# Turning attention outputs and expert products with transposing DMAs instead of TensorE

## What is computed

```python
x = x + 0.5 * ffn(layernorm(x))      # ternary weights, 128 -> 512 -> 128, relu
x = x + attn0(layernorm(x))          # rmsnorm, 16 heads of 64, causal, sigmoid gate per head
x = x + 0.5 * ffn(layernorm(x))
x = x + 0.5 * moe(layernorm(x))      # 8 experts, each token to its top 2
x = x + attn1(layernorm(x))          # layernorm, 16 heads of 64, causal
x = x + 0.5 * moe(layernorm(x))
```

## Time and profile before

| | us |
|---|---|
| median of three executions | 967.55 (967.09 to 970.55) |
| the profiled execution, its span from first to last instruction | 1000.9 |

### The profile page before, as it was taken

How to read it: one execution, slowest core, us unless ns; L and a number is a source line. 1 busy time by engine, 2 the same in 40 slices (tenths; PEclk the granted TensorE clock), 3 DMA queues, 4 the chain that set the end, 5 groups by cost and what they waited for, 6 DMA issues and landing times.

```text
span 1000.9 us, 33897 instructions
## 1 busy us (share of the span) xinstructions
PE 897.1 (90%) x13160; PEld 640.5 (64%) x13160; DVE 792.1 (79%) x2394; ACT 673.5 (67%) x1183; POOL 734.7 (73%) x685
## 2 busy tenths in 40 slices
PE   5789999999999879899987899999999985998884
PEld 3467676776777656566654676777677764666663
DVE  6889898888889877777656889888888887866563
ACT  6688888878877626556555787767767762545552
POOL 6789989889887745666545999878888883666662
PEclk9999999999999979999999999999999997999997
DMA  5201011010030001122111000000000001121222
GB/s 153 78 10 45 3 45 45 3 45 2 3 107 3 2 20 39 52 43 85 38 30 51 3 3 3 12 3 2 13 3 3 13 2 30 41 43 44 86 62 82
DMA packets 21118, 33.79 MB, mean 34 GB/s; under 512 B 4578, under 2 KB 10466, under 8 KB 20964
## 3 DMA queue, kind: packets, MB, share of 16 engines
q1 hardware_dynamic: 13728, 18.50, 5.9%
q0 software_dynamic: 5888, 12.07, 4.8%
q10 hardware_dynamic: 1348, 1.05, 0.3%
HBM read 22.44 MB, written 9.18 MB: 32 GB/s over the span
## 4 chain that ended last, share of the span: by engine, by line
PE 63%; DVE 18%; ACT 6%; issue 6%; POOL 3%; another core or an unknown queue 2%; DMA 1%; SPq 0%; POOLq 0%; DVEq 0%; ACTq 0%
PE ps L1698 8%; PE ps L1889 8%; PE ps L1700 8%; PE ps L1699 7%; DVE arena L1308 4%; PE ps L1919 3%; PE ps L2128 3%; PE ps L1853 3%; PE ps L1920 3%; PE ps L1921 3%; PE ps L2140 2%; PE ps L2141 2%; PE ps L2142 2%; PE ps L1864 2%
## 5 line engine op out<-in xcount | busy, mean ns | idle before, releaser
L784 POOL TENSOR_TENSOR arena<-arena 128x1024 f16<-128x1024 f32 x190 | 344.9, 1816 | 86.2 <-ACT arena L980 75.9
L1308 DVE CUSTOM_DVE_ANT_0 arena<-ps,mask_qk 128x512 bf16<-128x512 f32 (+3 forms) x512 | 224.4, 485 | 25.0 <-PE ps L1853 23.8
L972 ACT ACTIVATE arena<-ps,lift 128x1024 f32<-128x1024 f32 (+1 forms) x192 | 186.7, 972 | 85.0 <-PE ps L1899 82.2
L1889 PE MATMUL ps<-arena 64*128 64x512 f16 (+3 forms) x1536 | 148.5, 299 | 10.2 <-ACT arena L972 6.8
L835 POOL DMA_INDIRECT arena<-x_rows,arena x92 | 92.6, 1006 | 88.5 <-PE ps L2103 43.7
L1919 PE MATMUL ps<-arena 128*128 128x65 f16 x1280 | 130.9, 195 | 0.2 <-DVE arena L1332 0.2
L1920 PE MATMUL ps<-arena 128*128 128x64 f16 x1280 | 130.4, 193 | 0.0
L1921 PE MATMUL ps<-arena 128*128 128x65 f16 x1280 | 130.0, 194 | 0.0
L843 POOL DMA_INDIRECT y_rows<-arena x92 | 90.8, 987 | 49.0 <-ACT arena L1138 26.1
L1919 PEld LDWEIGHTS ps<-arena 128*128 128x128 f16 x1280 | 117.4, 98 | 8.4 <-issue 0.5
L1920 PEld LDWEIGHTS ps<-arena 128*128 128x128 f16 x1280 | 117.9, 99 | 0.2 <-issue 0.2
(11 more groups left out here) (288 smaller groups left out, 2695.9 us busy)
## 6 DMA issues: line engine op xcount, KB each, us to landing
stage<-in_L_ffn_W SPq DMA_DIRECT2D x4, 1024.0 KB, 5.3
arena<-y_rows SPq DMA_DIRECT2D x14, 256.0 KB, 3.6
x_rows<-XN SPq DMA_DIRECT2D x8, 256.0 KB, 2.1
arena<-x_rows,arena POOLq DMA_INDIRECT x92
y_rows<-arena POOLq DMA_INDIRECT x92
stage<-in_L_attn_Wkv SPq DMA_DIRECT2D x2, 512.0 KB, 8.3
X<-in_L_attn_tokens SPq DMA_DIRECT2D x3, 256.0 KB, 5.1
out_x<-X SPq DMA_DIRECT2D x3, 256.0 KB
```

The lines of the kernel that those rows point to most:

```text
L784: g.tensor_tensor(PL[:, b, :, cols], P32[:, :, cols], PH[:, b, :, cols], ALU.subtract).then_inc(s_pl, 1)
L972: a_.activation(P32[:, :, UNIT_AT[u]:UNIT_AT[u] + UNIT_W[u]], ps[:, 4:6, 0:UNIT_W[u]], ACT.Exp, bias=lift[:]).then_inc(s_ex_p, 1)
L1308: v_.tensor_tensor_reduce(masked[:, x, 0:w], ps[:, 2 + x, at:at + w], mask_qk[:, CH - w:CH], 1.0, NEG, ALU.add, ALU.max, accum_out=MX[:, i ...
L1889: mm(ps[:, 4 + x, at:at + w], keys, queries, start=(n_ == 0 and part == 0), stop=False)
```

## The change

1. Attention: `turn_outputs` goes. ACT `output_high` writes the high part of O32 into OS right at the turn's start, ahead of `exps(0)`; DVE `output_low` writes the rest, ahead of `maxima(0)`. SP issues one transposing DMA of 128x1024 float16 (both parts) into OT, which lies in T32; `project_out` waits for it.
2. Experts: `turned_product` goes. ACT and DVE split G32 itself into GS (three buffers), in step t-2; SP turns both parts with one transposing DMA into GT (four buffers, a semaphore each); the down product moves from lag 3 to lag 4. ACT takes `product_high` ahead of `gate`, DVE `product_low` ahead of `product`. The freed PSUM banks 3 and 4 double the banks of the up products.
3. The YS ring has eight buffers in place of four, in another place of the arena, and POOL waits for the last scatters before it writes there in the second attention.
4. SP's other DMAs are spread over the turns and steps, between the transposing ones.

```diff
-        GRING = 3
+        GRING = 4
+        SRING = 3
         XRING = 4
-        YRING = 4
+        YRING = 8
...
-        OTh = carve([CH], F16)
-        OTl = carve([CH], F16)
+        OS = carve([2, CH], F16)
+        OT = T32[:].bitcast(F16).rearrange("p (k i d) -> p k i d", k=2, i=TPB)
...
-        TLAGS = (0, 1, 2, 3)
+        DOWN_LAG = 4
...
+        def up_banks(t):
+
+            return 1 + 2 * (t % 2), 2 + 2 * (t % 2)
...  (SP)
+            def attention(a):
...
+                def body(t):
+                    o = items(t)[4]
+                    if o is not None:
+                        j = base + o
+                        sp.wait_ge(s_o_lo, j + 1)
+                        if j >= 1:
+                            sp.wait_ge(s_op_ps, j)
+                        sp.dma_start_transpose(OT.rearrange("p k i d -> p (k i) d"), OS.rearrange("p k c -> p (k c)")
+                                               ).then_inc(s_o_turned, 16)
+                    if a == 0 and t == 0:
+                        expert_block(0)
...
+            def moe(m):
+
+                for t in range(ETILES):
+                    w = ETILES * m + t
+                    sp.wait_ge(s_g_lo, w + 1)
+                    if t >= GRING:
+                        sp.wait_ge(s_y_ps, w - GRING + 1)
+                    sp.dma_start_transpose(GT[:, t % GRING].rearrange("p k f d -> p (k f) d"),
+                                           GS[:, t % SRING].rearrange("p k h -> p (k h)")
+                                           ).then_inc(s_g_turned[t % GRING], 16)
+                    if m == 0 and t == 4:
+                        rows_out(3, 2)
...
+                    if t == 31:
+                        results_in(m, 0)
...  (ACT)
+                    def output_high():
                         j = base + o
-                        act.wait_ge(s_ot_ps, j + 1)
-                        if o >= 1:
-                            act.wait_ge(s_op_ps, j)
-                        a_.activation(OTh, ps[:, 7, :], ACT.Copy).then_inc(s_oth_sb, 1)
+                        act.wait_ge(s_o_ev, j + 1)
+                        if j >= 1:
+                            act.wait_ge(s_o_turned, 16 * j)
+                        a_.activation(OS[:, 0], O32.rearrange("p a x d -> p (a x d)"), ACT.Copy).then_inc(s_o_hi, 1)
...
+                    if o is not None:
+                        output_high()
                     if s is not None:
                         exps(0)
...
                 def product_high(t, w):
-                    act.wait_ge(s_gt_ps, w + 1)
-                    if t >= GRING:
-                        act.wait_ge(s_y_ps, w - GRING + 1)
-                    a_.activation(GH[:, t % GRING].rearrange("p a b -> p (a b)"), ps[:, 3 + t % 2, :], ACT.Copy
-                                  ).then_inc(s_g_hi, 1)
+                    act.wait_ge(s_g32_rdy, w + 1)
+                    if t >= SRING:
+                        act.wait_ge(s_g_turned[(t - SRING) % GRING], moved(m, (t - SRING) % GRING, t - SRING + 1))
+                    a_.activation(GS[:, t % SRING, 0], G32[:, t % 2, :], ACT.Copy).then_inc(s_g_hi, 1)
...
-                run_tiles(m, (token_high, gate, product_high, result), carried)
+                run_tiles(m, ((token_high, 0), (product_high, 2), (gate, 1), (result, DOWN_LAG)), carried)
...  (DVE)
+                    if o is not None:
+                        output_low()
                     if m is not None:
                         maxima(0)
...
-                run_tiles(m, (token_low, product, product_low, None), carried)
+                run_tiles(m, ((token_low, 0), (product_low, 2), (product, 1)), carried)
...  (PE)
-                    def turn_outputs():
...
                     def project_out():
-                        pe.wait_ge(s_otl_sb, base + o + 1)
+                        pe.wait_ge(s_o_turned, 16 * (base + o + 1))
...
-                def turned_product(t, w):
...
                 def down(t, w):
                     g, e = t % GRING, offsets[t]
-                    pe.wait_ge(s_g_lo, w + 1)
+                    pe.wait_ge(s_g_turned[g], moved(m, g, t + 1))
...
-                run_tiles(m, (turned_token, up, turned_product, down), carried)
+                run_tiles(m, ((turned_token, 0), (up, 1), (down, DOWN_LAG)), carried)
```

More of the change, by code:

```diff
@@ L530, in macaron_block @@
         KEY_AT = {k: UNIT_AT[u] + at for u, unit in enumerate(EXP_UNITS) for k, at in unit}
-        TLAGS = (0, 1, 2, 3)
+        DOWN_LAG = 4
         OUT_LAG = 8
         def run_tiles(m, stages, carried):
-            for t in range(ETILES + TLAGS[-1]):
-                for f, lag in zip(stages, TLAGS):
-                    if f is not None and 0 <= t - lag < ETILES:
+            for t in range(ETILES + DOWN_LAG):
+                for f, lag in stages:
+                    if 0 <= t - lag < ETILES:
                         f(t - lag, ETILES * m + t - lag)
                 carried(m, t)
+        def up_banks(t):
+            return 1 + 2 * (t % 2), 2 + 2 * (t % 2)
         def second_weights(i):
@@ new lines, in rows_out, with results_in @@
+            def rows_out(n, c):
+                sp.wait_ge(s_ln_xn, NORM_NO[n, c])
+                at = c % HCH * CH
+                sp.dma_start(x_rows[c // HCH][at:at + CH].rearrange("(p t) d -> p t d", t=TPC),
+                             XN[:, TPC * c:TPC * (c + 1), :]).then_inc(s_x_rows[c // HCH], 16)
+            def results_in(m, h):
+                for k in range(YRING):
+                    sp.wait_ge(s_y_out[k], moved(m, k, HT * (h + 1), YRING))
+                for c in range(HCH * h, HCH * (h + 1)):
+                    for j in range(TOPK):
+                        at = j * TOK + c * CH
+                        sp.dma_start(Yt[:, c, j], y_rows[at:at + CH].rearrange("(p t) d -> p t d", t=TPC)
+                                     ).then_inc(s_y_got[c], 16)
@@ new lines, in attention @@
+            def attention(a):
+                base = a * ITEMS
+                def body(t):
[9 more added lines that the diff above has]
+                        expert_block(0)
+                    if a == 0 and t == 1:
+                        expert_block(1)
+                    if a == 0 and t in (6, 10, 14, 18):
+                        expert_block((t - 6) // 4 + 2)
+                    if a == 0 and t == 27:
+                        second_layer()
+                    if t in ROWS_OUT[a]:
+                        rows_out(*ROWS_OUT[a][t])
+                run_items(body, range(TURNS))
@@ L624, in _, with stored @@
[L624 to L633 removed]
+            x_out = out.rearrange("b (t p) d -> p (b t) d", p=P)
+            def stored(c):
+                sp.wait_ge(s_x_moe, TOPK * (NCH + c + 1))
+                sp.dma_start(x_out[:, TPC * c:TPC * (c + 1), :], X[:, TPC * c:TPC * (c + 1), :]
+                             ).then_inc(s_out_done, 16)
@@ new lines, in moe @@
+            def moe(m):
[9 more added lines that the diff above has]
+                        rows_out(3, 2)
+                    if m == 0 and t == 7:
+                        rows_out(3, 3)
+                    if m == 1 and t == 0:
+                        rows_out(5, 3)
+                    if t == 31:
+                        results_in(m, 0)
+                    if m == 1 and t == 38:
+                        stored(0)
+                    if m == 1 and t == 41:
+                        stored(1)
@@ L634, in _ @@
+            attention(0)
+            moe(0)
+            results_in(0, 1)
+            attention(1)
+            moe(1)
             end_loads()
@@ L773, in body @@
                         b = s & 1
+                        if a == 1 and s == 1:
+                            for k in range(YRING):
+                                pool.wait_ge(s_y_out[k], moved(0, k, ETILES, YRING))
                         for u in range(3 if s < ITEMS - 1 else 2):
@@ L1032, in body @@
                             k_high()
-                    if o is not None:
-                        turned_high()
                     if s is not None:
@@ L1146, in _ @@
             for k in range(YRING):
-                act.wait_ge(s_y_out[k], moved(1, k, ETILES))
+                act.wait_ge(s_y_out[k], moved(1, k, ETILES, YRING))
             for j in range(TOPK):
@@ L1389, in body @@
                         counts_half(a, 0)
-                    if o is not None:
-                        turned_low()
                     if t == TURNS - 3:
@@ L1955, in body @@
                             project_k()
-                    if o is not None:
-                        turn_outputs()
                     if s is not None:
```

124 lines of the change are left out of this document (45 added, 79 removed).

## The result

The changed kernel takes 1027.27 us (median of four, 1026.21 to 1031.41) where the one before takes 967.88 beside it: a ratio of 1.062, interval 1.060 to 1.064. It is 59 us slower; the forecast was 45 us faster.

The account below looks back on a forecast made before the run. It took PE as nearly full, with DVE close behind in attention and POOL in the moes. 19.5 - 2.5 + 34.5 - 5 = 46.5 us, scaled to 45, gave 922 us; its own range was 900 to 945, the overall range 893 to 980.

Parts of the forecast that it names:

- I cost the difference at nothing on both engines: Attention: ACT and DVE splits reading SBUF cost the same as before, within 0.1 us a turn on DVE, 6 us in all.
- no further gain: Attention: splits at the turn's start delay DVE's maxima(0) by 0.6 us, but DVE's work sum is the same; nothing further counted.
- The saving of 19.5 us: Attention: without PE's turn, DVE idle above 0.80 us goes, 0.37 and 0.24 us a turn over 32 turns each.
- The 34.5 us of the moes: Moes: POOL's 2.56 us a tile becomes the bound; 9.0 and 6.5 us in middle windows, 19 us in other intervals.
- I scale by 0.967: Whole kernel: the 46.5 us saving of the 1000.9 us profiled span scaled to the 967.55 us median, giving 45 us.
- 4.5 us are there, against 3.6: Moes: 4.5 us of other work cover the transposing DMA before the down product, against 3.6 us taken for it.
- PE idle before the down product until a DMA: Moes: a named sign that the forecast is wrong, PE standing idle before the down product until a DMA.
- The clock: "nothing": Moes: even at a granted clock of 0.88 PE would need 2.4 us a tile, still under POOL; no cost counted.
- the attention transfer: Attention: the transposing DMA takes 3.6 us and is hidden behind 4.7 us, except 1.3 us at each of two drains.
- the pace of the queue: Moes: each transposing DMA holds the queue 2.3 us or less, from 1024 pieces of 256 bytes on 16 engines.
- the transfer is slower than a tile: Moes, rival, chance 0.20: at 4.4 us a transfer PE's down product waits; 85 us slower, 1053 us.
- The third rival: Attention and moes, chance 0.04: DVE's split ahead of maxima(0) holds PE as the transposes did, POOL and routing set the moes; 967 us.

Follow-up runs that it names:

- low_on_act: Attention part alone on the kernel before, with ACT writing both parts of OS and DVE having no output split; 1016.96 us, ratio 1.007 to the kernel before.
- moe_part: The changed kernel with its attention part undone; experts, YS ring and SP's order stay changed; 973.07 us, ratio 1.004 to the kernel before.
- plain_moe: moe_part with ACT fetching rows by plain DMAs from the fifth tile on, in place of POOL's gathers; 969.79 us, ratio 1.001 to the kernel before.
- before_again: The kernel before, unchanged, profiled a second time: 968.51 us, profiled span 966.7 us.
- plain_half: plain_moe with the transposing DMA halved, only high parts turned; 958.55 us, ratio 0.955 to the kernel before.
- dummy_dma: The kernel before plus one transposing DMA of 128x1024 a turn that nobody reads; 1009.01 us, ratio 1.000.

## Why the prediction was wrong

**The step that failed first: "I cost the difference at nothing on both engines".** It priced the splits by shape, 0.69 us, between ends of 0.1 us a turn. The runs show 1.14 us on average and up to 2.36. The row that stood nearest by shape, L1361, reads PSUM; no row of before was asked which operands lie in SBUF and what POOL does meanwhile, though POOL was busy 179 of 200 us in the earlier trace rows. In the right column of the table above this is 36 us. On ACT the step was right: its split took 0.63 us from SBUF and 0.59 from PSUM.

**The second: the order of the turn's start, "no further gain" and no loss.** It counted a later `maxima(0)` as harmless, as DVE does the same sum of work. With the split from PSUM the early order costs 14 us: PE's next products wait until DVE has reduced the maxima before, its scores until ACT has made the exponentials, and both come later.

**The saving of 19.5 us.** DVE's idle time above 0.80 us a turn didn't go when PE's turn went, not even in `low_on_act`, where DVE has less to do than in the forecast: it is idle (200 - 162.0)/21 = 1.81 and (200 - 161.4)/22 = 1.75 us of a turn there, and the turns are as long as before. That the chain from `maxima(2)` over `outputs(1)` to `evacuate` keeps its 0.80 us was right, and it is why every added tenth on DVE counts. What became of the other tenths isn't isolated; the rows show ACT as the next that is late.

**The 34.5 us of the moes.** POOL as the next bound, at 2.56 us, was right for the middle of the second moe: in 850:900 of `moe_part` POOL waits for little but "issue", and the tiles come (899.1 - 849.8)/19 = 2.59 us apart. (`plain_moe`, without the gathers, has 2.54 there, so it wasn't the only bound.) The size was wrong: 9 + 6.5 us for the middle windows and 19 for the other intervals were measured from an execution whose moes are 36 us longer than in before_again, and "I scale by 0.967" spread over the program an excess that lay wholly in the stage where the saving was counted. By the prediction's own sum the middle windows of before_again, of 17 and 19 tiles, hold 50 - 17 x 2.56 = 6.5 and 50 - 19 x 2.56 = 1.4 us, 8 in place of 15.5; and the first of them still has 17 tiles in `moe_part`.

**The cover for the DMA in the moes, "4.5 us are there, against 3.6".** It took each transfer by itself. In the changed kernel the DMA share is 0.75 in 900:950, and `down` waits for the transfer 19.8 us in 19 times. That is the sign "PE idle before the down product until a DMA" that the prediction named. That these waits alone held the moes isn't shown, as `plain_half`, where they are fewer, has the gathers off POOL as well.

**The clock: "nothing".** The granted clock stays at 1.00 in long windows, and falls to 0.57 and 0.50 behind PE gaps of 4.1 and 1.5 us in `plain_moe`. The mean of 0.88 over 46 us in the earlier trace rows hid that: in that window it is 1.00 up to 987 us and 0.50 from 991 on.

**Right were** the attention transfer (2.8 us to landing against a cover of 4.7, and `dummy_dma` at 1.000), the pace of the queue (packets of q1: (178464 - 13728)/156 = 1056 for each transposing DMA, and 27.5% of 1024.1 us less 5.9% of 1000.9 us, over 156, 1.43 us each of all 16 engines, under the 2.3 taken), and setting aside the Trainium skill's 1309 ns a block ("VectorE: DVE Perf Modes", The three transpose paths), which would have made 10.5 us of a DMA. The rivals didn't decide: "the transfer is slower than a tile" got the sign of the result and not its place. The third rival, DVE's split holding PE as the transposes did, was the nearest; it priced the hold at what the transposes cost, so at no change.

## What to carry to other kernels

Before you let an instruction read SBUF that read PSUM, look what GpSimd does at that time: on the engine that sets the pace, price it at its own duration plus what can be left of the GpSimd operation that it falls into, and try it late and early in the loop. Where the profiled execution is not the length of the median, find by stages where the difference lies before you scale a saving. And of work taken from a busy engine, ask what chain ends last in a loop: here PE at 98% gave nothing back.

## What the runs showed of the hardware

The transposing DMA of 128x1024 float16 (256 KB, inside SBUF) keeps SP's queue for 1.23 us where a plain one of 256 KB (x_rows) takes 0.32 in the kernel before and 0.57 in the changed one. It lands after 2.8 us at the median in the attentions, and is made of 1056 packets; one of half the size in `plain_half` keeps the queue for 1.19 us. Rows after (ns min/median/max, first and last start):

```profile
L632 SPq DMA_TRANSPOSE T<-arena x64: 1232/1232/2267, 68.2 to 871.7; - x64
...
L675 SPq DMA_TRANSPOSE arena<-arena x92: 1232/1233/2738, 398.2 to 1007.2; - x92
```

At 1.43 us of all 16 DMA engines it moves some 180 GB/s, by my estimate; with one for each tile beside the rows' own transfers, the DMA share of `plain_moe` reaches 1.0 for some us at a time. And in two executions of the kernel before the attentions agree to a microsecond, and its moes are 20 and 16 us apart (155.9 and 139.8, 136.1 and 123.5).
